# Key copies, context rows and the first text gain moved in the order of four engines

## The reference

```python
# 1: cross attention, FiLM, S4D, feed-forward
xn = layernorm(x)                                     # no gain or bias
scores = (xn @ Wq) . (ctx @ Wk) / sqrt(32)            # 4 heads, 128 x 2048 each
topv, topi = top_k(scores, 32); probs = softmax(topv) # zero elsewhere
c_t = (mean over heads of probs) @ (ctx @ Wv)
h = layernorm(xn) * g_in + b_in
h = h * (1 + gate * scale_in) + gate * shift_in       # from c_t @ W_film_in + b
y = s4d(h) * (1 + gate * scale_out) + gate * shift_out
xt = xn + y;  xt = xt + gelu(layernorm(xt) @ W1 + b1) @ W2 + b2
x = x + layernorm(xt)
# 2: banded self attention    # 3: mixture of 16 experts, top 2, capacity 80
```

## Time and profile before

| | us |
|---|---|
| median of 3 runs | 776.59 (776.24 to 779.22) |
| the profiled execution | 776.36 |
| its span in the profile | 774.5 |
| PE busy in the span | 676.0 (87%) |
| DVE, ACT, POOL busy | 366.7, 268.4, 234.1 |

### The profile page before, as it was taken

How to read it: one execution, slowest core, us unless ns; L and a number is a source line. 1 busy time by engine, 2 the same in 40 slices (tenths; PEclk the granted TensorE clock), 3 DMA queues, 4 the chain that set the end, 5 groups by cost and what they waited for, 6 DMA issues and landing times.

```text
span 774.5 us, 10077 instructions
## 1 busy us (share of the span) xinstructions
PE 676.0 (87%) x3848; PEld 316.6 (41%) x3848; DVE 366.7 (47%) x1179; ACT 268.4 (35%) x564; POOL 234.1 (30%) x146
## 2 busy tenths in 40 slices
PE   4967669888378799999999999999699999999997
PEld 1423235334244354444444444455544333333343
DVE  5998769978998235570003350534661111001114
ACT  1866868779688110013210002444111001111010
POOL 2499668858977910000000000000140000000012
PEclk9977676868569999999999999999699999999999
DMA  9971320802706750014014023002958999999924
GB/s 296 289 271 52 108 83 2 271 1 76 291 0 222 213 239 19 1 41 176 0 50 167 0 82 135 1 1 74 361 201 311 389 379 344 373 373 371 384 81 135
DMA packets 63521, 132.94 MB, mean 172 GB/s; under 512 B 8368, under 2 KB 18544, under 8 KB 62960
## 3 DMA queue, kind: packets, MB, share of 16 engines
q1 hardware_dynamic: 59072, 122.91, 44.1%
q0 software_dynamic: 1920, 6.29, 2.8%
q10 hardware_dynamic: 2480, 3.08, 1.2%
HBM read 121.86 MB, written 8.32 MB: 168 GB/s over the span
## 4 chain that ended last, share of the span: by engine, by line
PE 67%; ACT 10%; DVE 7%; POOL 6%; DMA 4%; issue 3%; SPq 2%; DVEq 0%; POOLq 0%
PE PS L1696 7%; PE PS L1671 7%; PE PS L1492 7%; PE PS L1512 7%; PE PS L1410 6%; PE PS L1264 4%; PE PS L1529 4%; PE PS L1691 4%; PE PS L1676 4%; PE PS L1297 3%; DMA AR<-in_ctxT 3%; DVE AR L1010 2%; PE PS L1314 2%; PE PS L1526 2%; SPq L290 2%
## 5 line engine op out<-in xcount | busy, mean ns | idle before, releaser
L422 POOL TENSOR_TENSOR RS<-VE,CST 128x1 f32<-128x1 f32 (+1 forms) x18 | 11.2, 623 | 267.6 <-DVE VE L919 265.3
L1297 PE MATMUL PS<-AR,WK 128*128 128x512 f32 x96 | 55.8, 738 | 17.2 <-DMA AR<-in_ctxT 17.1
L956 DVE MAX8 KA<-AR 128x8 f32<-128x64 f32 x512 | 66.4, 211 | 0.8 <-ACT AR L607 0.8
L1235 DVE COPY AR<-PS 128x512 f32<-128x512 f32 (+1 forms) x9 | 5.9, 668 | 124.3 <-PE PS L1264 124.3
L574 POOL DMA_INDIRECT AR<-expert_rows,SLU x8 | 8.4, 1050 | 180.9 <-DMA expert_rows<-XT 178.8
L1696 PE MATMUL PS<-AR,TT 128*32 128x512 f32 x512 | 59.5, 593 | 1.4 <-issue 1.3
L1314 PE MATMUL PS<-AR,QT 32*128 32x512 f32 x128 | 45.1, 790 | 16.8 <-ACT AR L607 13.5
L1671 PE MATMUL PS<-AR 128*32 128x512 f32 x512 | 58.0, 594 | 1.1 <-ACT AR L870 0.6
L1492 PE MATMUL PS<-TT,AR 128*128 128x512 f32 (+2 forms) x144 | 55.5, 546 | 3.3 <-ACT TT L798 3.3
L1410 PE MATMUL PS<-AR 128*128 128x512 f32 x128 | 56.1, 594 | 0.9 <-ACT AR L770 0.6
L1512 PE MATMUL PS<-AR 128*128 128x512 f32 x128 | 55.5, 593 | 0.9 <-ACT AR L807 0.9
(11 more groups left out here) (293 smaller groups left out, 1197.4 us busy)
## 6 DMA issues: line engine op xcount, KB each, us to landing
AR<-in_w SPq DMA_DIRECT2D x32, 2048.0 KB, 12.4
AR<-in_ctxT SPq DMA_DIRECT2D x16, 768.0 KB, 7.6
AR<-in_ctx SPq DMA_DIRECT2D x16, 768.0 KB, 7.8
AR<-in_W SPq DMA_DIRECT2D x2, 4096.0 KB, 12.9
token_rows<-AR SPq DMA_DIRECT2D x1, 2560.0 KB, 10.1
X<-in_x SPq DMA_DIRECT2D x2, 1024.0 KB, 5.5
AR<-AR POOLq DMA_DIRECT2D x8, 256.0 KB, 3.4
AR<-in_W_film_in SPq DMA_DIRECT2D x4, 512.0 KB, 10.5
```

What stands on the lines that cost most here:

```text
L956: last = eng.max(CAND[i % 2][:, n, :], s[:, n * G // NCH:(n + 1) * G // NCH])
L1297: last = mm(PS[:, 4 + n % 2, :], WK[:, j, :], CXT[slot][:, j, :], start=j == 0, stop=j == KV - 1)
```

## The change

Only orders change; no operation is added or removed, apart from the two of gains(0), which go from POOL to DVE. The exponentials of a pair are split: `exponentials(m)` keeps the small operations, `weight(i)` is the large one. Then:

- ACT, passes 3 and 5: the last two key copies of a batch, until now at the end of passes 2 and 4, come behind both weights of the next pass.
- ACT, attended(0): from the end of pass 4 to behind these copies in pass 5. Attended(1): from the end of pass 6 to between weight(12) and weight(13) of pass 7, with the first two context row copies of batch 2.
- ACT, pass 7: attended(2) ahead of step_sizes(3).
- ACT, pass 8: text_norm(0) ahead of exponentials(7), the copies of the context text between weight(14) and weight(15).
- gains(0): from POOL, ahead of its last two head sums, to DVE, ahead of last_powers(), which thereby waits for text_norm(0).
- DVE: modulate(0) ahead of diagonal(3). PE: film_in(0) ahead of lags(3).

PE's order in the passes is unchanged. In both kernels attended(b) is the last call of PE's even pass, ahead of the scores of the next pass.

```diff
--- before.py
+++ after.py
@@ -534,9 +534,6 @@
                 q, k = divmod(i, 4)
                 if k == 0 and 1 <= q < 4:
                     powers(q - 1)
-                if i == NT:
-                    eng.wait_ge(S_["ld_vin"], 32)
-                    gains(0)
                 add_head(i - 2)
                 if k == 2 and 1 <= q < 4:
                     fractions(q)
@@ -619,11 +616,13 @@
                 for i, v, a in pair:
                     last = link.put(eng.activation(a[:, 3:4], a[:, 2:3], ACT.Identity, bias=a[:, 0:1], scale=-1.0))
                 link.after(last)
-                for i, v, a in pair:
-                    if i >= 2:
-                        eng.wait_ge(S_["added"], sums_until(i - 2))
-                    eng.activation(W[i % 2], SC[i % NSC], ACT.Exp, bias=a[:, 3:4], scale=SCALE)\
-                       .then_inc(S_["e_done"], 1)
+
+            def weight(i):
+
+                if i >= 2:
+                    eng.wait_ge(S_["added"], sums_until(i - 2))
+                eng.activation(W[i % 2], SC[i % NSC], ACT.Exp, bias=SM[:, i % 4, 3:4], scale=SCALE)\
+                   .then_inc(S_["e_done"], 1)
 
             def attended_rows(b, part):
 
@@ -679,6 +678,18 @@
                 for k in range(LB):
                     last = eng.activation(MGN[:, k, :], al, ACT.Exp, scale=float(k))
                 last.then_inc(S_["trig"], 1)
+
+            def text_norm(b):
+
+                eng.activation(XL[:, b, :], XT[:, b, :], ACT.Identity, bias=NB2[:, b:b + 1],
+                               scale=RS2[:, b:b + 1]).then_inc(S_["xn"], 1)
+
+            def text_context():
+
+                for k in range(KD):
+                    eng.wait_ge(S_["ct_ps"], k + 1)
+                    eng.activation(CTT[:, k, 0:3 * T], PS[:, k, 0:3 * T], ACT.Copy, scale=MG[:, 0:1])\
+                       .then_inc(S_["ct_sb"], 1)
 
             def text_columns(b, bank):
 
@@ -713,12 +724,27 @@
             eng.preload_act_table_set("natural_log_exp_and_others")
             for m in range(NPH + 1):
                 q, late = divmod(m, 2)
+                if m == NPH:
+                    eng.wait_ge(S_["nb"], 1)
+                    eng.wait_ge(S_["masked"], NT - 3)
+                    text_norm(0)
                 if 2 <= m:
                     exponentials(m - 1)
+                    weight(2 * m - 2)
+                    if m == NPH - 1:
+                        attended(1)
+                        attended_rows(2, (0, 1))
+                    if m == NPH:
+                        text_context()
+                    weight(2 * m - 1)
                 if late:
+                    if q and q + 1 < B:
+                        context_keys(q + 1, (2, 3))
+                    if q == 2:
+                        attended(q - 2)
                     if m + 1 < NPH:
                         scores(m + 1, (0, 1))
-                    if q:
+                    if 1 <= q < 3:
                         attended_rows(q - 1, (0, 1))
                     if m + 1 < NPH:
                         scores(m + 1, (2, 3))
@@ -727,10 +753,10 @@
                     if q:
                         sines(q)
                     lag_sizes(q)
+                    if q == 3:
+                        attended(2)
                     if q:
                         step_sizes(q)
-                    if q == 3:
-                        attended(2)
                 elif m < NPH:
                     if m == 2:
                         step_sizes(0)
@@ -743,9 +769,10 @@
                         step_turns(q)
                     else:
                         exponentials(0)
-                    if q + 1 < B:
-                        context_keys(q + 1, (2, 3))
+                        weight(0)
+                        weight(1)
                     if m == 0:
+                        context_keys(1, (2, 3))
                         for b in range(1, B):
                             text_columns(b, (5, 7)[b % 2])
                         sines(0)
@@ -754,21 +781,7 @@
                     if m == 2:
                         eng.wait_ge(S_["ld_small"], 16 * 7)
                         link(eng.activation(TM[:, :], TM8[:, :], ACT.Copy))
-                    if q >= 2:
-                        attended(q - 2)
-
-            def text_norm(b):
-
-                eng.activation(XL[:, b, :], XT[:, b, :], ACT.Identity, bias=NB2[:, b:b + 1],
-                               scale=RS2[:, b:b + 1]).then_inc(S_["xn"], 1)
-
-            eng.wait_ge(S_["nb"], 1)
-            eng.wait_ge(S_["masked"], NT - 3)
-            text_norm(0)
-            for k in range(KD):
-                eng.wait_ge(S_["ct_ps"], k + 1)
-                eng.activation(CTT[:, k, 0:3 * T], PS[:, k, 0:3 * T], ACT.Copy, scale=MG[:, 0:1])\
-                   .then_inc(S_["ct_sb"], 1)
+
             for b in range(1, B):
                 text_norm(b)
             eng.wait_ge(S_["ld_bf"], 32)
@@ -1094,6 +1107,10 @@
                     diagonal(q - 1)
                 thresholds(m, found)
                 settle(m)
+            eng.wait_ge(S_["xn"], 1)
+            eng.wait_ge(S_["ld_vin"], 32)
+            link(tt(XL[:, 0, :], XL[:, 0, :], G_IN, mul))
+            link(tt(XL[:, 0, :], XL[:, 0, :], B_IN, add))
             last_powers()
             masked(NT - 2)
             masked(NT - 1)
@@ -1101,7 +1118,8 @@
             def modulate(b):
 
                 xl = XL[:, b, :]
-                eng.wait_ge(S_["xlg"], b + 1)
+                if b:
+                    eng.wait_ge(S_["xlg"], b)
                 eng.wait_ge(S_["fi_ps"], 2 * b + 1)
                 link(tt(US, PS[:, 0, :], BFI[:, 0, :], add))
                 link(tt(xl, xl, US, mul))
@@ -1109,9 +1127,9 @@
                 link(tt(xl, PS[:, 1, :], xl, add))
                 tt(xl, xl, BFI[:, 1, :], add).then_inc(S_["x2"], 1)
 
-            diagonal(3)
             eng.wait_ge(S_["gate"], 4)
             modulate(0)
+            diagonal(3)
             eng.wait_ge(S_["ld_k"], 16)
             tt(KRAW[:, :, 0], KRAW[:, :, 0], DSK[:, :], add).then_inc(S_["kraw"], 1)
             eng.wait_ge(S_["spec"], 3)
@@ -1450,8 +1468,8 @@
                 last.then_inc(S_["ct_ps"], 1)
             eng.wait_ge(S_["ld_far"], 16)
             eng.wait_ge(S_["ld_wfi"], 16 * KD)
+            film_in(0)
             lags(3)
-            film_in(0)
             transform(0)
             attended_rows(3, range(4))
             context_rows(3)
```

## The result

| us | before | after |
|---|---|---|
| median of 20 runs each | 776.83 (775.36 to 779.52) | 779.78 (777.12 to 785.28) |
| ratio to before | | 1.0037, 95% interval 1.0026 to 1.0048 |
| the profiled execution, its span | 776.36, 774.5 | 779.57, 777.8 |
| PE busy, mean granted clock | 676.0, 0.916 | 679.6, 0.912 |

The change costs 2.9 us (2.0 to 3.7). This is real, but smaller than the 0.5% that I had called slower. The forecast of 781.8 was 2.0 too high; the time of rival A, 778.8, was 1.0 too low, so the number alone cannot tell the two apart. The traces can.

The account below looks back on a forecast made before the run. TensorE's chain from about 264 us was taken to pass any shift of its start to the end; shifts carried through passes 3, 5, 7 and the hand-over came to +5.4, so 776.36+5.4=781.8 us, range 776.0 to 786.0.

Parts of the forecast that it names:

- rival A: Pass 5 costs nothing, as scores run at the higher clock or attended(0) is not in the way: +2.4, 778.8 us; chance 0.17.
- Pass 3: Key copies leave the way of exponentials(2); the end of the pass moves by -1.1 us, bounds 0 and -2.5.
- Pass 5: Weight(8) starts earlier, but late attended(0) holds TensorE's first score chunks; third chunk at 171.1 instead of 169.22: +1.9 us.
- Pass 7: Context_rows(2) start late, attended(2) waits for them ahead of step_sizes(3); weight(14) at 243.3 against 239.00: +4.3 us.
- The hand-over: VectorE waits for text_norm(0), its gains meet GpSimd's products; GpSimd's last head sum ends at 265.8, before 260.36.
- the exclusion: At the hand-over, DVE and GpSimd shut each other out for operations reading two SBUF tensors; gains of 0.7 us take turns.
- Rival B: Faster: gains take 1.4 us on VectorE, GpSimd's 6.5 leave the chain: -4.4 to -5.7, about 771 us; chance 0.12.
- Rival C: Slower still: TensorE stays at its lower clock through the rows of batch 3: +3.7, 785.5 us; chance 0.16.
- Rival D: The moves do not act, since what they reorder is not late: 776.5 us; chance 0.05.
- The S4D kernel's store: Leaves SP at about 262 instead of 250.46 behind the moved diagonal(3); even with 13.0 us again, cost 0 (0 to +1).

Follow-up runs that it names:

- the first two runs: Changed kernel with TensorE's attended(0) behind two score chunks (776.23 us, ratio 0.9979); changed kernel with ScalarE's attended(0) back at the end of pass 4 (775.96 us, 0.9984).
- passes 3 and 5 alone: Kernel before with only the late key copies of passes 3 and 5 and attended(0) behind them on ScalarE: 781.87 us, ratio 1.0035.
- Pass 7 alone: Kernel before with only attended(1) and two row copies between weight(12) and weight(13), and attended(2) ahead of step_sizes(3): 781.67 us, ratio 1.0041.

## Why the prediction was right or wrong

All differences are behind the mark, against before.

- **Pass 3**: forecast -1.1; the first table load of pass 3 is 1.0 earlier (44.63 behind the mark for 45.63). Right: in the ten traces with the keys late it starts at 43.9 to 44.8, in the three without at 45.0 to 46.1.
- **Pass 5**: forecast +1.9; sine table load +2.1. Weight(8) at 158.5 was forecast, 157.84 (158.6 with the mark's 0.8) measured; TensorE idle for CC 5.00, the transposes 0.90, the clock behind them 0.50. Right, and shown by the first two runs and by passes 3 and 5 alone. Rival A, whose time was nearer than mine, is refuted in its mechanism: the table load came at 177.72, not before 176.4.
- **Pass 7**: forecast +4.3 for weight(14), measured +4.25. Context_rows(2) began at 222.77 (223.6 with the 0.8; forecast 223.35). The wait ahead of attended(2) was 0.73, not 1.3, since sines and lag sizes ended 0.65 later than my 234.5. That the fractions lost 2.06 us to masked(12) I had not told as a cause. It hides behind context_rows(2) here and comes out in the run with step_sizes(3) first. Pass 7 alone confirms that the pass costs (+4.2 in its trace, 0.41% in its times), but no run parts its three edits cleanly.
- **The hand-over**: two gains of over 2 us each, DVE idle 5.16 for text_norm(0), masked(14) ending at 251.76 (252.6; forecast 252.8). Right, and the exclusion is shown by the run without GpSimd's step products. The mis-sized term is the last one: from masked(14) the two sums took 12.3 us instead of 13.0. The last sum came +4.5 behind before, not +5.4. Rival B needed the exclusion to be avoided; it was not. Rival C, the lower clock in the rows of batch 3, did not come: context_rows(3) took 10.59 us in both kernels. Rival D, that the moves do not act, falls with the rows above.
- **The S4D kernel's store** left SP at 260.89 (forecast 262) and took 7.9 us instead of 13.0. TensorE had its term in time, at 277.69. Cost 0, right.
- **From 4.5 to 2.9 us.** The spans of the profiled executions differ by 3.3: 4.5, less 0.8 for the earlier mark and 0.4 behind context_rows(3). The medians have 2.9. The forecast's sum had 5.4, of which 0.9 is the hand-over's size; the rest, 1.6, lies ahead of and behind the places the change touches, and no run here says why.
- **Chances**: I gave 0.56 to slower by over 0.5% and 0.32 to within it. It is 0.37% slower. The mechanism held, and the most likely class did not come: the cost lay below the bound of 0.5%, the sum of 5.4 us above it.

The Trainium skill (SBUF — State Buffer, Who interferes with whom) has the pair of ports shared by VectorE and GpSimd as an exclusive lock. For a VectorE instruction with two SBUF inputs beside a GpSimd one that reads SBUF, the same page's Summary says that the second one to issue fully blocks until the first finishes. The traces agree: 4.41 or 4.20 us for whoever was second by 0.16 and 0.30 us, 2.35 for the first. The advice there, to schedule whichever is off the critical path, did not decide here, because both engines' work was on it.

## What to carry to other kernels

When you move a step later on one engine, look in every other engine's program for what is queued behind its consumer: with the copies moved alike, three transposes, 0.9 us in all but waiting for their copy, made the third score chunk 2.1 us later than before when they stood in front of the first two, and it was 2.0 earlier when they stood behind them. Where two engines exclude each other, price a moved instruction by whom it will meet; here removing it let the next one meet the same partner, and only removing the partner helped. Before shortening a hand-over, list all that the next engine has in program order in front of it (here the gate's bias, modulate, transform): in five of these runs it was transform(0) and no longer the sums that the transposes waited for, by 1.1 to 5.6 us.

## What was not expected of the hardware

- Being late by 0.16 to 0.30 us decides 2 us: masked(12) took 4.20 us when it came 0.30 behind GpSimd's product, and 2.35 when it came first, and the product 4.41.
- Only some operations were shut out. In after, L1124 and L1127, which read PSUM and SBUF, took 0.68 and 0.69 us beside GpSimd's sums; L1125 and L1128, which come behind each of them and read SBUF twice, took 2.13 and 1.99.
- After idle time TensorE could lose in clock what had been gained: 16 transposes with their copies in 4.46 us at 0.59 against 3.18 at 1.00; the text context 11.04 at 0.71 against 7.98 at 1.00. That took 1.3 and 3.1 us back from edits made to save waiting elsewhere.
- The same idle time did not always cost the same. In seven traces TensorE idled 9.15 and then 1.68 us (within 0.01) ahead of the context rows of batch 2, and their 32 matmuls took 10.59, 10.59, 12.26, 12.28, 12.40, 13.51 and 13.58 us, at a granted clock of 1.00 down to 0.78. No row here shows what decides it, so a single trace cannot settle a difference of this size.
